# Node stage of a two-layer graph network: a ring of four blocks for the loaded tables, self rows loaded three blocks later, stores eight steps behind

## The chip, the cores and the metric

The kernel runs on one core of one Trainium2 chip. The metric is the device time of one execution in microseconds (us); for the kernel before it is the median of three runs.

## The reference

There are 12,500 nodes with 128 features each and 200,000 edges sorted by destination. Layer 0 adds to x a self branch and a neighbour branch, each relu(row @ W.T + b), normalised over its 128 columns, scaled and shifted; a layer norm follows. Layer 1 gathers projected node rows along the edges, weights them by a small network on the edge attributes, sums them by destination, and mixes them with a projection of the node's own row:

```
def _branch(x, W, b, scale, offset, idx):
    h = relu(x @ W.T + b)
    return (h - mean(h)) * s * rsqrt(var(h) + EPS) + o

# layer 0
feat_neigh = segment_sum(edge_val[:, None] * x[src], dst)
x = layernorm(x + _branch(x, W_self, ..., 0) + _branch(feat_neigh, W_neigh, ..., 1))

# layer 1
sc = x projected by W_sc (own row)       f = x projected by W_l1
g = f[src];  weight = silu-network(edge_scalars)
m = segment_sum(weight * g * edge_attr, dst)
x = layernorm(x + cos(angle(m)) * sc + sin(angle(m)) * (m projected by W_l2))
```

What is changed sits between the two layers: from the summed neighbour rows and the self rows to the new x, sc and f.

## The kernel before, in words

The work is five stages, each a block in which every engine runs its own program; between stages all engines meet at a barrier. (1) Setup and the self stage: 25 blocks of 500 nodes; x plus the self branch goes to `base_scratch` in HBM. (2) The neighbour stage: 196 groups of 1024 edges, summed by scatter-add (indirect DMAs issued by POOL) into four tables in HBM, `sums_scratch0` to `3`. (3) The node stage, lines 718 to 904: the part that the change touches. (4) The edge stage: 196 groups, gathers issued by POOL, sums kept in the SBUF tile `table`. (5) The final stage, 25 blocks.

The node stage treats 25 blocks (NB) of 500 nodes, laid out as 125 partitions by 4 rows (CB) by 128 columns. Every engine runs a software pipeline with `sweep`: eight steps written out, a loop of steps 8 to 23 unrolled by four (UN), the rest written out. In step s an engine works on block s for the first part of the chain and on earlier blocks for the later parts:

- SP, step b: four loads of block b, one from each table, into `t_in` (L761), after a wait on `m_sum` for block b-2; one load of the self rows into `b_in` (L763), after a wait on `m_y` for block b-4; then, for block b-6, a wait on `m_pk` and two stores: x and sc together to `xs_scratch` (L767), f to `f_scratch` (L769).
- PE, step s: adds the four tables of block s by 32 matmul rows against the identity, which also transpose (L799, counts up `m_sum`); the neighbour matmul of block s-1 (L807, L810); the transposes of x of block s-4 (L818, needs `m_x1`); the projection of block s-5 (L825, `m_f`).
- ACT, step s: copies and the relu of those results, and the square roots.
- DVE, step s: statistics of h of block s-2 and of y of block s-3 (after `m_y`), then the two scaled copies of sc and f of block s-5 into `pack` (L894, counts up `m_pk`), then centring of h of block s-2 and of y of block s-3 (L877; the latter writes x into `pack` and counts up `m_x1`).
- POOL, step s: clears `table` once (L776), then for block s-3 scales h (L783) and adds the self rows (L787, `m_y`).

The DMAs of the stage all are issued by SP, in the order of its program; SP stops at each wait. The tile `pack` is a ring of four blocks: before DVE writes x of block m into it in step m+3 (L903), it waits until the stores of block m-4 have landed (L902, semaphores `pk_st`). `done(e, signal, m, n)` makes engine e wait until the signal has been counted up for block m-n; `uses` waits for a ring slot's DMAs. Helpers record some lines: L85, L87 and L89 are the steps of the reciprocal square root.

```
uses(dve, pk_st[i2], r2, 32)
centre(m2, y[:, i2 % 2, :, :], pack[:, i2, :, 0, :], 1).then_inc(m_x1, 1)
```

`dst0` (a copy of the edge destinations, last used in the neighbour stage) and `zeros` (last used in the self stage) are SBUF tiles that stay allocated to the end of the kernel.

Of the kernel before, what the change touches and what calls it, by code (L numbers as in the profile page):

```python
# [13 lines left out]
F32 = mybir.dt.float32  # L14
# [5 lines left out]
P = 128  # L20
N = 12500
E = 200000
D = 128
MUL = 32
EF = 64
TH = 4
# [7 lines left out]
NH = 2 * NSG  # L34
# [3 lines left out]
NP = 125  # L38
CB = 4
NB = N // (NP * CB)  # L40
# [4 lines left out]
NTAB = 4  # L45
NPAD = 99 * P
UN = 4


def sweep(eng, body, first, last, lo, hi):  # L50

    for s in range(first, lo):
        body(s, s // UN, s % UN)
    with eng.Fori(lo // UN, hi // UN) as q:  # L54
        for j in range(UN):
            body(q * UN + j, q, j)
    for s in range(hi, last):
        body(s, s // UN, s % UN)


def at(s, q, j, back):

    return s - back, q + (j - back) // UN, (j - back) % UN
# [7 lines left out]
def done(eng, signal, step, back=0):  # L71

    if not isinstance(step, int) or step >= back:
        eng.wait_ge(signal, step - back + 1)
# [18 lines left out]
def graph_layers(nc, a, out):  # L93
    with ExitStack() as ctx:
        def sb(name, shape, dt=F32):
            return ctx.enter_context(nc.sbuf_tensor(name, shape, dt))

        def sem(name):
            return ctx.enter_context(nc.semaphore(name))

        def bank(name, shape, scope):
            return scope.enter_context(nc.psum_tensor(name, shape, F32))

        base_d = nc.dram_tensor("base_scratch", (N, D), F32, kind="Internal").ap()
# [3 lines left out]
        sums_d = [nc.dram_tensor(f"sums_scratch{i}", (NPAD, D), F32, kind="Internal").ap() for i in range(NTAB)]  # L108
# [2 lines left out]


        dstf = sb("dstf", [P, NH, TH])
        dst0 = sb("dst0", [P, NH, TH])
        base0 = sb("base0", [P, NH])
        base = sb("base", [P, NH])
        base_i = sb("base_i", [1, NH], I32)
# [6 lines left out]
        ident = sb("ident", [P, P])  # L124
# [9 lines left out]
        attr = sb("attr", [NP, NB * CB])  # L134
        attr_s = sb("attr_s", [NP, NB * CB])
        ZPART = NPAD * D // P // (24 // UN)
        zeros = sb("zeros", [P, ZPART])


        with ExitStack() as s0:  # L140
            def tmp(name, shape, dt=F32):
                return s0.enter_context(nc.sbuf_tensor(name, shape, dt))
# [189 lines left out]
        def rows_of(t, b):  # L332
            return t[bass.ds(b * BN, BN), :].rearrange("(c p) d -> p c d", p=NP)

        def live(b):
            return not isinstance(b, int) or 0 <= b < NB
# [161 lines left out]
        with ExitStack() as s2:  # L498
# [24 lines left out]
            ps_n = [bank(f"ps_n{i}", [W, TH, P], s2) for i in range(2)]  # L523
# [191 lines left out]

        table = sb("table", [P, 2, NT])
        with ExitStack() as s3:
            def tmp(name, shape, dt=F32):  # L720
                return s3.enter_context(nc.sbuf_tensor(name, shape, dt))
            b_in = tmp("b_in", [NP, UN, CB, D])
            t_in = tmp("t_in", [NP, 2, NTAB, CB, D])
            nT = tmp("nT", [P, 2, CB, NP])
            h = tmp("h_m", [NP, 2, CB, D])
            y = tmp("y_m", [NP, 2, CB, D])
# [10 lines left out]
            ps_n = bank("ps_mn", [P, CB, P], s3)  # L737
            ps_t = bank("ps_mt", [P, CB, P], s3)
            ps_f = [bank(f"ps_mf{i}", [NP, CB, 2 * D], s3) for i in range(2)]
            b_ld = [sem(f"m_b_ld{i}") for i in range(UN)]  # L740
            pk_st = [sem(f"m_pk_st{i}") for i in range(UN)]
            t_ld = [sem(f"m_t_ld{i}") for i in range(UN)]
            m_sum = sem("m_sum")
# [6 lines left out]
            m_cen, m_hs, m_y, m_x1 = sem("m_cen"), sem("m_hs"), sem("m_y"), sem("m_x1")  # L750
# [3 lines left out]
            with nc.Block() as block:  # L754
                @block.sync
                def _(sp):
                    def body(b, q, j):
                        if live(b):
                            done(sp, m_sum, b, 2)
                            for i in range(NTAB):  # L760
                                sp.dma_start(t_in[:, j % 2, i, :, :], rows_of(sums_d[i], b)).then_inc(t_ld[j], 16)  # L761
                            done(sp, m_y, b, UN)
                            sp.dma_start(b_in[:, j, :, :], rows_of(base_d, b)).then_inc(b_ld[j], 16)  # L763
                        m, r, i = at(b, q, j, 6)
                        if live(m):
                            done(sp, m_pk, m)
                            sp.dma_start(rows_of(xs_d, m),  # L767
                                         pack[:, i, :, 0:2, :].rearrange("p c g d -> p c (g d)")).then_inc(pk_st[i], 16)
                            sp.dma_start(rows_of(f_d, m), pack[:, i, :, 2, :]).then_inc(pk_st[i], 16)  # L769
                    sweep(sp, body, 0, NB + 6, 8, 24)  # L770
                    for i in range(UN):
                        sp.wait_ge(pk_st[i], 32 * len(range(i, NB, UN)))

# [16 lines left out]
                @block.tensor  # L790
                def _(pe):
                    def body(s, q, j):
                        b = s
                        if live(b):
                            uses(pe, t_ld[j], q + 1, 16 * NTAB)
                            done(pe, m_nT, b, 1)
                            for c in range(CB):
                                for i in range(NTAB):
                                    last = pe.matmul(ps_n[:, c, 0:NP], t_in[:, j % 2, i, c, :], ident[0:NP, 0:NP],  # L799
                                                     start=(i == 0), stop=(i == NTAB - 1))  # L800
                            last.then_inc(m_sum, 1)
                        b, r, i = at(s, q, j, 1)
                        if live(b):
                            k = i % 2
                            done(pe, m_nT, b)
                            done(pe, m_relu, b, 2)
                            pe.matmul(ps_m[k][:, :, :], ones[0:1, 0:NP], bias4[:, 1, :, :], start=True, stop=False,  # L807
                                      skip_group_check=True)
                            for c in range(CB):
                                last = pe.matmul(ps_m[k][:, c, :], nT[:, k, c, :], neigh_wT[:, :],  # L810
                                                 start=False, stop=(c == CB - 1), skip_group_check=True)
                            last.then_inc(m_mm, 1)
                        m, r, i = at(s, q, j, 4)
                        if live(m):
                            done(pe, m_x1, m)
                            done(pe, m_x1T, m, 1)
                            for c in range(CB):
                                last = pe.transpose(ps_t[:, c, 0:NP], pack[:, i, c, 0, :], ident[0:NP, 0:NP])  # L818
                            last.then_inc(m_tr, 1)
                        m, r, i = at(s, q, j, 5)  # L820
                        if live(m):
                            done(pe, m_x1T, m)
                            done(pe, m_pk, m, 2)
                            for c in range(CB):
                                last = pe.matmul(ps_f[i % 2][:, c, :], x1T[:, i % 2, c, :], node_w[:, :], start=True, stop=True)  # L825
                            last.then_inc(m_f, 1)
                    sweep(pe, body, 0, NB + 5, 8, 24)
# [434 lines left out]
```

## Time and profile before

| | us |
|---|---|
| median of 3 runs | 6106.29 (6099.2 to 6108.52) |
| the profiled execution's own time | 6105.86 |
| its span | 6104.0 |
| node stage: first load issued, last byte moved | 3300.24, between 3810 and 3812 |
| edge stage: first SP issue | 3814.29 |

| engine | busy us over the span | share |
|---|---|---|
| PE | 3681.6 | 60% |
| DVE | 3027.1 | 50% |
| ACT | 979.0 | 16% |
| POOL | 4237.4 | 69% |

The profile's page has the span in 40 equal slices; the node stage lies in slices 22 to 25. A row of the timeline gives start, duration, engine, line, operation, tiles, and how many like instructions are merged in it (then the duration reaches from the first start to the last end). SPq stands for DMA issues by SP: the duration is what the issue took on SP, not the transfer. The bracket at a row's end is idle time of the engine before it and what ended it.

### The profile page before, as it was taken

Reading aid. Unit: us, or ns where it says so; the run is one execution under the profiler, and the core shown is the slowest. Engines: PE = TensorE matmul, PEld = TensorE weight load, DVE = VectorE, ACT = ScalarE, POOL = GpSimd, SP = SyncE. Lnnn points to the kernel's source line nnn. Section 1 sums busy time; section 2 is a strip of 40 time slices with the busy share of each in tenths; the row PEclk is TensorE's granted clock in tenths of the full one; section 3 lists DMA queues with packets and bytes.
Section 4 is the critical chain, followed back from the end, with each engine's and each line's share of the span. In section 5 each row is a group of like instructions: output and inputs, shape, how many; then the busy total and the mean of one; then the engine's idle time right before and its main releaser. Section 6 shows DMA issues by size and latency. Waiting matters only on the chain. (4 is left out here: it accounts for less than half of the span.)

```text
span 6104.0 us, 77354 instructions
## 1 busy us (share of the span) xinstructions
PE 3681.6 (60%) x19065; PEld 3070.4 (50%) x19065; DVE 3027.1 (50%) x11110; ACT 979.0 (16%) x2389; POOL 4237.4 (69%) x3326
## 2 busy tenths in 40 slices
PE   3455554555445555555453554788888888888841
PEld 2233333333333333333332443788888887887841
DVE  3355555555555555555552544444444444444445
ACT  0122222222222222222220100111111111111100
POOL 1258888888888888888886111777777777777743
PEclk9987666677776676677766777777777777777765
DMA  6356666666666666666664333333333333333322
GB/s 115 139 110 107 107 111 110 107 107 107 109 112 107 107 107 113 109 107 107 107 110 69 103 105 91 80 78 78 76 78 78 76 78 78 76 78 79 76 65 88
DMA packets 841278, 587.30 MB, mean 96 GB/s; under 512 B 333361, under 2 KB 737809, under 8 KB 838161
## 3 DMA queue, kind: packets, MB, share of 16 engines
q0 software_dynamic: 275968, 205.72, 25.4%
q1 hardware_dynamic: 560433, 354.96, 21.1%
q10 hardware_dynamic: 4832, 26.13, 1.1%
q8 instruction: 16, 0.26, 0.0%
q14 instruction: 29, 0.23, 0.0%
HBM read 374.34 MB, written 212.14 MB: 96 GB/s over the span
## 5 line engine op out<-in xcount | busy, mean ns | idle before, releaser
L704 POOL DMA_INDIRECT sums_scratch<-vals,to_i x1568 | 2453.6, 1565 | 513.7 <-issue 358.8
L968 POOL DMA_INDIRECT fg<-f_scratch,src_e x1568 | 1561.7, 996 | 514.5 <-issue 477.5
L650 PE MATMUL ps_n<-same,hot 128*40 128x128 f32 x3136 | 700.2, 417 | 1408.1 <-issue 1406.5
L650 PEld LDWEIGHTS ps_n<-same,hot 128*40 128x40 f32 x3136 | 559.2, 185 | 1512.6 <-issue 1449.2
L997 PE MATMUL ps_eu<-hot,prod 128*128 128x120 f32 x3136 | 906.6, 384 | 0.0
L995 PEld LDWEIGHTS ps_eu<-hot,prod 128*128 128x128 f32 x3136 | 637.2, 249 | 345.6 <-DVE prod L1047 257.2
L995 PE MATMUL ps_eu<-hot,prod 128*128 128x40 f32 x3136 | 629.5, 292 | 290.6 <-DVE prod L1047 290.6
L617 DVE TENSOR_TENSOR to_i<-away,srcf 128x8 int32<-128x8 f32 x196 | 32.9, 168 | 1304.0 <-POOLq L68 1303.8
L1046 DVE TENSOR_TENSOR prod<-ps_ew,fg 128x256 f32<-128x256 f32 x392 | 164.4, 419 | 986.3 <-DMA fg<-f_scratch,src_e 936.2
L997 PEld LDWEIGHTS ps_eu<-hot,prod 128*128 128x128 f32 x3136 | 633.2, 250 | 0.0
L604 DVE SCALAR_TENSOR_TENSOR junk<-srow_s,srcf,lower 128x128 f32<-128x128 int32 x1568 | 581.7, 435 | 0.0
L984 PE MATMUL ps_ew<-fc_w,hid_e 128*128 128x256 f32 x1568 | 498.6, 475 | 22.6 <-DMA hid_e<-hid_scratch 22.6
L663 PEld LDWEIGHTS ps_v<-xw_s,near 40*128 40x128 f32 x3136 | 365.1, 188 | 199.3 <-issue 106.9
L1019 ACT COPY sums_a<-ps_eu 32x80 f32<-32x80 f32 x784 | 170.0, 217 | 1822.3 <-PE ps_eu L997 1815.6
L678 ACT COPY near<-ps_n 40x512 f32<-40x512 f32 x196 | 113.5, 579 | 1910.4 <-PE ps_n L650 1910.4
L984 PEld LDWEIGHTS ps_ew<-fc_w,hid_e 128*128 128x128 f32 x1568 | 368.8, 248 | 81.8 <-DMA hid_e<-hid_scratch 23.0
L663 PE MATMUL ps_v<-xw_s,near 40*128 40x128 f32 x3136 | 402.5, 279 | 1.3 <-ACT vals L689 1.3
L592 DVE TENSOR_SCALAR same<-srow_s,srcf 128x128 f32<-128x128 int32 x1568 | 396.6, 335 | 5.1
L1047 DVE TENSOR_TENSOR prod<-ps_ew,fg 128x768 f32<-128x768 f32 x392 | 371.4, 947 | 0.0
L597 DVE TENSOR_SCALAR hot<-iota_f,rel,ew_s 128x40 f32<-128x40 f32 x1568 | 357.1, 341 | 0.0
L799 PE MATMUL ps_mn<-ident,t_in 125*128 125x125 f32 x800 | 147.0, 366 | 266.1 <-DMA t_in<-sums_scratch 266.1
L783 POOL TENSOR_TENSOR y_m<-h_m,vecs 125x512 f32<-125x512 f32 x25 | 31.5, 1261 | 394.1 <-DVE h_m L877 394.1
(192 smaller groups left out, 4365.6 us busy)
## 6 DMA issues: line engine op xcount, KB each, us to landing
srow_s<-in_src SPq DMA_DIRECT2D x196, 512.0 KB
e_s<-in_edge_attr SPq DMA_DIRECT2D x196, 256.0 KB, 3.8
hid_scratch<-hid SPq DMA_DIRECT2D x196, 256.0 KB, 3.6
hid_e<-hid_scratch SPq DMA_DIRECT2D x196, 256.0 KB
sums_scratch<-zeros ACTq DMA_DIRECT2D x24, 1056.0 KB, 3.9
sums_scratch<-vals,to_i POOLq DMA_INDIRECT x1568, 3.4
fg<-f_scratch,src_e POOLq DMA_INDIRECT x1568
t_in<-sums_scratch SPq DMA_DIRECT2D x100, 250.0 KB
```

The lines of the kernel that those rows point to most:

```text
L592: last = dve.tensor_scalar(same[:, k, t, :], rows[:, t // TH, t % TH, :], srcf[:, t:t + 1], None, ALU.is_equal)
L597: last = dve.tensor_scalar(hot[:, k, t, :], iota_f[:, 0:W], rel[:, t // TH, t % TH:t % TH + 1], ew_s[:, j, t:t + 1], ALU.is_equal, ALU.mult)
L604: last = dve.scalar_tensor_tensor(out=junk[:, t, :], in0=rows[:, t // TH, t % TH, :], scalar=srcf[:, t:t + 1], in1=lower[:, :], op0=ALU.is ...
L650: last = pe.matmul(ps_n[t // TH][:, t % TH, :], hot[:, k, t, :], same[:, k, t, :], start=True, stop=True)
L663: last = pe.matmul(ps_v[t // TH][:, t % TH, :], near[:, k, t, :], xw_s[:, i, t // TH, :], start=True, stop=True)
L704: pool.indirect_dma_start(out=sums_d[i], out_offset=bass.IndirectOffsetOnAxis(ap=to_i[:, j, t:t + 1], axis=0), in_=vals[:, j, t, :], in_of ...
L968: pool.indirect_dma_start(out=fg[:, j, t, :], out_offset=None, in_=f_d, in_offset=bass.IndirectOffsetOnAxis(ap=src_s[:, j, t:t + 1], axis= ...
L984: last = pe.matmul(ps_w[k][:, 2 * t:2 * t + 2, :, :], hid[:, j, t, :], fc2_w[:, :], start=True, stop=True)
L995: pe.matmul(ps_u[k][:, hf, 0, :], prod[:, k, t, 0, :], hot[:, k, t, 0, :], start=(t == 0), stop=False, skip_group_check=True)
L997: last = pe.matmul(ps_u[k][:, hf, 1:4, :], prod[:, k, t, 1, :], hot[:, k, t, 1:4, :], start=False, stop=(t == TS - 1), skip_group_check=True)
L1019: act.copy(sums_a[MUL * c:MUL * (c + 1), i % 2, :, :], ps_u[i % 2][MUL * c:MUL * (c + 1), :, c, :])
L1047: last = dve.tensor_tensor(prod[:, k, :, g, MUL:D].rearrange("p t (d u) -> p t d u", d=3), ps_w[k][:, :, 2 + g, None, :].to_broadcast([P, ...
```

## The change

`t_in` becomes a ring of four blocks instead of two, so the wait in front of the table loads of block b is for the sum of block b-4 instead of b-2. The load of the self rows in step b is now that of block b-3 (its wait: `m_y` of block b-7, four before it). The stores in step b are those of block b-8 instead of b-6, so SP's sweep has two steps more. `pack` and `b_in` keep their four blocks. `dst0` and `zeros` move into a scope that is closed before `table` is allocated, which makes room for the larger `t_in`; this moves SBUF addresses and no instruction. Beside SP's program one index of PE's matmul changes (L799, after: L803).

```diff
-        dst0 = sb("dst0", [P, NH, TH])
...
-        zeros = sb("zeros", [P, ZPART])
+        early = ctx.enter_context(ExitStack())
+        zeros = early.enter_context(nc.sbuf_tensor("zeros", [P, ZPART], F32))
+        dst0 = early.enter_context(nc.sbuf_tensor("dst0", [P, NH, TH], F32))
...
+        early.close()
         table = sb("table", [P, 2, NT])
...
-            t_in = tmp("t_in", [NP, 2, NTAB, CB, D])
+            t_in = tmp("t_in", [NP, UN, NTAB, CB, D])
...
                     def body(b, q, j):
                         if live(b):
-                            done(sp, m_sum, b, 2)
+                            done(sp, m_sum, b, UN)
                             for i in range(NTAB):
-                                sp.dma_start(t_in[:, j % 2, i, :, :], rows_of(sums_d[i], b)).then_inc(t_ld[j], 16)
-                            done(sp, m_y, b, UN)
-                            sp.dma_start(b_in[:, j, :, :], rows_of(base_d, b)).then_inc(b_ld[j], 16)
-                        m, r, i = at(b, q, j, 6)
+                                sp.dma_start(t_in[:, j, i, :, :], rows_of(sums_d[i], b)).then_inc(t_ld[j], 16)
+                        m, r, i = at(b, q, j, 3)
+                        if live(m):
+                            done(sp, m_y, m, UN)
+                            sp.dma_start(b_in[:, i, :, :], rows_of(base_d, m)).then_inc(b_ld[i], 16)
+                        m, r, i = at(b, q, j, 8)
                         if live(m):
                             done(sp, m_pk, m)
                             sp.dma_start(rows_of(xs_d, m),
                                          pack[:, i, :, 0:2, :].rearrange("p c g d -> p c (g d)")).then_inc(pk_st[i], 16)
                             sp.dma_start(rows_of(f_d, m), pack[:, i, :, 2, :]).then_inc(pk_st[i], 16)
-                    sweep(sp, body, 0, NB + 6, 8, 24)
+                    sweep(sp, body, 0, NB + 8, 8, 24)
...
-                                    last = pe.matmul(ps_n[:, c, 0:NP], t_in[:, j % 2, i, c, :], ident[0:NP, 0:NP],
+                                    last = pe.matmul(ps_n[:, c, 0:NP], t_in[:, j, i, c, :], ident[0:NP, 0:NP],
```

Only SP's program is reordered. At the start of the node stage SP's rows read, before (xs_scratch and f_scratch are the stores, t_in the table loads, b_in the self rows):

```order
L761 DMA t_in<-sums_scratch 125x4x128 x4
L763 DMA b_in<-base_scratch 125x4x128
L761 DMA t_in<-sums_scratch 125x4x128 x4
L763 DMA b_in<-base_scratch 125x4x128
L761 DMA t_in<-sums_scratch 125x4x128 [waits m_sum]
L761 DMA t_in<-sums_scratch 125x4x128 x3
L763 DMA b_in<-base_scratch 125x4x128
```

and now:

```order
L763 DMA t_in<-sums_scratch 125x4x128 x16
L767 DMA b_in<-base_scratch 125x4x128
L763 DMA t_in<-sums_scratch 125x4x128 [waits m_sum]
L763 DMA t_in<-sums_scratch 125x4x128 x3
L767 DMA b_in<-base_scratch 125x4x128
```

The table loads of four blocks now go out before the first self row and before the first wait. At the end of the stage, from step 24 (the last table loads) on, SP's rows read before:

```order
L761 DMA t_in<-sums_scratch 125x4x128 [waits m_sum]
L761 DMA t_in<-sums_scratch 125x4x128 x3
L763 DMA b_in<-base_scratch 125x4x128 [waits m_y]
L767 DMA xs_scratch<-pack 125x4x256 [waits m_pk]
L769 DMA f_scratch<-pack 125x4x128
L767 DMA xs_scratch<-pack 125x4x256 [waits m_pk]
L769 DMA f_scratch<-pack 125x4x128
```

with five more such pairs of stores behind them, seven in all; and now:

```order
L763 DMA t_in<-sums_scratch 125x4x128 [waits m_sum]
L763 DMA t_in<-sums_scratch 125x4x128 x3
L767 DMA b_in<-base_scratch 125x4x128 [waits m_y]
L771 DMA xs_scratch<-pack 125x4x256 [waits m_pk]
L773 DMA f_scratch<-pack 125x4x128
L767 DMA b_in<-base_scratch 125x4x128 [waits m_y]
L771 DMA xs_scratch<-pack 125x4x256 [waits m_pk]
L773 DMA f_scratch<-pack 125x4x128
```

with two more groups of three and five pairs of stores behind them: four self rows and nine pairs of stores stand at or behind step 24 where there were one and seven.

## Rows read from the trace of the kernel before

**Rows 1.** The page, part 2: DMA busy tenths and GB/s in 40 slices.

```profile
DMA  6356666666666666666664333333333333333322
GB/s 115 139 110 107 107 111 110 107 107 107 109 112 107 107 107 113 109 107 107 107 110 69 103 105 91 80 78 78 76 78 78 76 78 78 76 78 79 76 65 88
```

**Rows 2.** DMA issues of the node stage: count and KB each.

```profile
t_in<-sums_scratch SPq DMA_DIRECT2D x100, 250.0 KB
xs_scratch<-pack SPq DMA_DIRECT2D x25, 500.0 KB
b_in<-base_scratch SPq DMA_DIRECT2D x25, 250.0 KB
f_scratch<-pack SPq DMA_DIRECT2D x24, 250.0 KB
```

**Rows 3.** Stretches: engines' busy time (instructions), granted PE clock, DMA share, GB/s.

```profile
3302.00:3380.00 78.00, 45.32 (x234) 40.82 (x235) 21.31 (x98) 7.60 (x16) 26.81 (x7) 0.68 0.36 104
3420.00:3740.00 320.00, 162.84 (x864) 139.69 (x864) 153.15 (x591) 29.23 (x80) 42.90 (x34) 0.76 0.35 104
3750.00:3810.00 60.00, 24.41 (x86) 18.13 (x85) 32.23 (x113) 4.84 (x14) 7.58 (x6) 0.68 0.25 76
```

**Rows 4.** Timeline of SP: table loads of steps 1, 2, then of 8 and 24.

```profile
3309.01 9.75 SPq L761 DMA_DIRECT2D t_in<-sums_scratch  x4
3321.34 9.75 SPq L761 DMA_DIRECT2D t_in<-sums_scratch  x4
...
3410.07 11.51 SPq L761 DMA_DIRECT2D t_in<-sums_scratch  x4
...
3725.36 11.55 SPq L761 DMA_DIRECT2D t_in<-sums_scratch  x4
```

**Rows 5.** SP's waits in the node stage: total us, times, longest.

```profile
SPq L767 <- DVE pack L894: 50.1, 7, 10.5
SPq L763 <- POOL y_m L787: 17.4, 9, 2.5
SPq L761 <- PE ps_mn L799: 5.8, 2, 3.6
```

**Rows 6.** Timeline of the end of the stage: SP, PE, DVE.

```profile
3742.84 5.94 PE L799 MATMUL ps_mn<-ident,t_in 125*128 125x125 f32 x32 [9.67 <-DMA t_in<-sums_scratch]
...
3754.40 0.26 SPq L767 DMA_DIRECT2D xs_scratch<-pack  x1
...
3758.94 1.11 DVE L877 TENSOR_SCALAR pack<-y_m,mv_m,rs_m 125x128 f32<-125x128 f32 x4
...
3765.90 0.26 SPq L767 DMA_DIRECT2D xs_scratch<-pack  x1
...
3770.43 1.12 DVE L877 TENSOR_SCALAR pack<-y_m,mv_m,rs_m 125x128 f32<-125x128 f32 x4
...
3776.78 0.26 SPq L767 DMA_DIRECT2D xs_scratch<-pack  x1
...
3788.35 0.27 SPq L767 DMA_DIRECT2D xs_scratch<-pack  x1
...
3789.03 1.12 DVE L877 TENSOR_SCALAR pack<-y_m,mv_m,rs_m 125x128 f32<-125x128 f32 x4
...
3796.06 0.26 SPq L767 DMA_DIRECT2D xs_scratch<-pack  x1
...
3798.03 3.42 SPq L767 DMA_DIRECT2D xs_scratch<-pack  x1
...
3812.26 0.36 DVE L938 COPY base<-base 128x392 f32<-128x392 f32 x1 [14.26 <-PEq L754]
```

**Rows 7.** Stretches of 2 us, same columns as rows 3.

```profile
3750.00:3752.00 2.00, 2.00 (x16) 1.91 (x16) 0.00 (x0) 1.07 (x4) 0.00 (x0) 1.00 0.12 36
...
3754.00:3756.00 2.00, 1.17 (x9) 0.95 (x8) 1.86 (x9) 0.00 (x0) 0.00 (x0) 1.00 0.13 35
3810.00:3812.00 2.00, 0.00 (x0) 0.00 (x0) 0.00 (x0) 0.00 (x0) 0.00 (x0) 0.50 0.23 68
```

## The prediction

> **What bounds the kernel now.** I read the page's slices first, then the node stage by its issues, stretches, SP's waits and its timeline. In the slices the node stage lies where GB/s reads 103, 105 and 91 [rows 1]: about 8% of the span, and the only part whose instructions the change reorders. Its transfers are 25 blocks of four table loads, one self load, one x-and-sc store and one f store, 250 KB each but for the first store's 500 KB [rows 2]. In units of 250 KB (256,000 bytes) that is 8 units a block and 200 in all (the missing 25th f store lies past the stretch that was asked).
>
> The rate is the same whatever the engines do: 104 GB/s while there are only loads, and 104 GB/s over 320 us with stores among them, at a DMA share of 0.36 and 0.35, while PE is busy for half the time [rows 3]. The issues say the same. With loads alone a step of 5 units takes 3321.34 - 3309.01 = 12.33 us, 2.466 us a unit. With stores, 16 steps of 8 units take 3725.36 - 3410.07 = 315.3 us, 19.7 us a step, 2.463 us a unit [rows 4]. So the queue of SP's transfers never runs dry there, and bytes set the pace, not the number of buffers.
>
> A share near 0.36 of 16 engines also says that few engines carry these transfers. The Trainium skill (DMA: Bandwidth & Descriptors, section on why a DMA increments its semaphore by 16 and not by 1) gives a DMA the largest number of engines up to 16 that divides the slowest dimension of both sides, and takes the lowest-numbered ones on the queues of SP and ACT. For 125 partitions that is 5, always the same; 5/16 is 0.31, so the trace nearly agrees, and by that rule too no order of the loads changes the rate.
>
> Only the end of the stage is not full. From 3750 to 3810 the DMAs move 76 GB/s [rows 3]; at 104 those bytes would need 60 × 76/104 = 43.8 us, so they stand still for 16.2 us. The gaps are there to see: 36 GB/s from 3750, 35 from 3754 [rows 7]. The reason is in SP's waits: 50.1 us in 7 waits of the stores for DVE's `pack` [rows 5]. When the last loads are out, six blocks have still to be stored, and `pack` of blocks 19 to 22 comes only every 11 us: 3754.40, 3765.90, 3776.78, 3788.35, then 3796.06 and 3798.03 [rows 6], where a pair of stores takes three units, 7.4 us. So in the tail the chain of the engines is the limit, with holes of 3 to 4 us in the DMA queue, and the last two pairs end the stage: bytes stop near 3811.3 (68 of 104 GB/s in the last 2 us [rows 7]), DVE goes on at 3812.26 [rows 6].
>
> **What the change does, part by part.** Bytes, instructions of PE, ACT, DVE and POOL: unchanged. Cost 0; SP issues the same 175 DMAs, two more empty half-steps. The moved SBUF tiles have no row here; I take 0, and the nearest bound is the spread of the runs, 9 us in all, between 3 us faster and 3 us slower for the median of three.
>
> *Steady steps.* The wait for the sum before the table loads cost 5.8 us in two instances and the wait before the self load 17.4 us in nine [rows 5], all while earlier transfers were still draining at 104 GB/s. Their removal gives 0. That is the point at which deeper buffers usually are expected to pay, and here they can't, below the 2.463 us a unit.
>
> *The end of the stage.* At the end of step 24 SP had issued 182 of the 200 units before (100 table, 25 self, 19 pairs of 3). It now has issued 100 + 22 + 17 × 3 = 173; nine pairs of stores and three self loads follow. I count from one anchor: bytes stop first near 3750.7 [rows 7], with unit 182, and unit n is now done at T(n) = 3750.7 - 2.463 × (182 - n), if the queue doesn't run dry. The last table load is unit 169 instead of 178: T = 3718.7 instead of 3740.8. PE started its sum at 3742.84 [rows 6], 2.0 us behind, so it starts near 3720.7, 22 us earlier. The tail of the engines now runs while the queue still has stores for 31 units, 76 us.
>
> *The wait that takes the place of the old one.* `pack` keeps four slots. DVE may write x of block m only when the stores of block m-4 have landed (L902), and SP now issues those in the step after the one in which DVE wants to write, two steps later than before. Behind that wait in DVE stand the next step's statistics and `pack`; PE's transposes wait for x, and ACT, POOL and PE's next sum stand behind these. In steady steps it costs nothing at the end: DVE waits for the end of SP's step m+4, PE then does the projection and DVE the `pack` of the block before, about 6 us on, while SP wants that `pack` two steps (39 us) later. In the tail I work it out with two lengths of rows 6: from x written (3758.94 + 1.11 = 3760.05) to the next store's issue (3765.90) 5.9 us, and from there to x of the next block (3770.43 + 1.12 = 3771.55) 5.7 us; a load or store lands 2.0 us behind T, and writing x takes 1.1.
> - x of 20: stores of 16 done at T(173) = 3728.5, so x at 3731.6, `pack` of 19 at 3737.5.
> - x of 21: 3743.2 by DVE (3741.5 by the ring, T(177)); `pack` of 20 at 3749.1; x of 22 at 3754.8, `pack` of 21 at 3760.7; x of 23 at 3766.4, `pack` of 22 at 3772.3; x of 24 1.8 us on (3788.35 to 3790.15 before), `pack` of 23 at 3780.0, and of 24 two us on.
> - The queue wants the stores of 20 at T(185) = 3758.1, of 21 at 3765.5, of 22 at 3772.9, of 23 at 3780.3, of 24 at 3787.7. Against 3749.1, 3760.7, 3772.3, 3780.0 and 3782.0, with some 1 us from issue to the first bytes, there is a hole of 0 to 0.7 us at blocks 22 and 23, and none else. Self rows of 22 to 24 now come between the stores, the last at T(182) = 3750.7, before y of 24 is due.
> So the last byte is at T(200) = 3795.0 plus up to 0.7, against 3811.3: 15.6 to 16.3 us earlier. Should the landing be 3 us later than taken, another 3 are lost; should the chain be 0.5 us a step shorter, nothing is gained, because bytes are the floor.
>
> *Start.* `pack` of 0 is wanted in step 8 instead of 6, and t_in of steps 0 to 3 is issued in one go; nothing ran dry there before [rows 3]: 0.
>
> *Sum.* 6105.86 (the profiled execution; 0.43 below the median) - 15.5 = 6090.4; on the median 6106.29 - 15.5 = **6090.8 us**. The edge stage begins 15.5 us earlier and keeps its length.
>
> The Trainium skill (DMA: Bandwidth & Descriptors, the anatomy of one DMA) puts most of a DMA's fixed 2 us into the receipt of the last write, heaviest for HBM. That speaks against this change, since DVE now waits on stores to HBM. The trace has 2.0 us for a load, and under 1 us from the last stored byte to DVE's L938; by the page's 2.0 the steps above stay as they are.
>
> **The rivals.**
> - *The tail stays chain-bound.* If stores land late or the chain is 1 to 2 us longer in each of its five steps, the last `pack` slips by 5 to 10 us beyond the slack and the gain shrinks to 5 to 12 us: 6094 to 6101. For it: the margins at blocks 22 and 23 are under 1 us, and the granted clock of PE is 0.68 over the tail against 0.76 in the loop [rows 3], so a tail that starts elsewhere may meet another clock. Against it: four table loads take SP 9.75 us to issue, as long as their transfers [rows 4], so SP runs ahead of the queue by some transfers, and the steps I took are those of the slower tail.
> - *Nothing gained.* The holes only move: the self rows between the stores, or a ring of `pack` that empties the queue in the loop as much as it fills the tail. 6106. Against it: 39 us of slack.
> - *Slower.* The `pack` ring closes a loop: stores landed, x of the block four on, PE, `pack`, stores. One turn is 1.1 + 5.9 + 7.4 + 2 + 1 = 17.4 us and passes three blocks; it decides only if a turn covers one block, for example because SP, standing in the wait for `pack`, holds back the table loads that PE needs first. Then each of 17 steps would add the issue-to-landing 2 us that no transfer hides: +34 - 15.5 = +18, 6125.
>
> **How the numbers follow.** Forecast 0.78, chain-bound tail 0.12, nothing 0.05, slower 0.05. The bound of 0.2% (12.2 us, what a measurement of this kernel can tell from no change) lies 3.3 us from the forecast, and medians of these runs wander by some 3: of the forecast's 0.78, 0.73 is faster and 0.05 the same; of the chain-bound tail 0.01 is faster and 0.11 the same. Faster 0.74, same 0.21, slower 0.05. The range: 16.3 plus the wander of 6 us below gives 6084; above, it takes in half of the chain-bound tail and reaches 6100.
>
> **What would show it.** Right: 104 GB/s without a gap until about 3795; PE's last sum near 3721; SP's waits for `pack` nearly gone; the first SP issue of the edge stage near 3798 to 3799; steps of 19.7 us in the loop; a new wait of DVE's L877 for stores in steps 7 to 24, without effect. Wrong: any dip of GB/s before 3770 (the ring of `pack` binds), holes of over 1 us after it (the chain still ends last), a step in the loop unlike 19.7 us, or an edge stage that changes its length.

## The result, and the profile after

| | before | after |
|---|---|---|
| median of 18 runs each, us | 6105.99 (6099.2 to 6110.41) | 6114.27 (6112.22 to 6130.2) |
| ratio after / before, 95% interval | | 1.0016 (1.0009 to 1.0023) |
| span of the profiled execution | 6104.0 | 6110.6 |
| up to the first table load of the node stage | 3300.2 | 3300.7 |
| node stage (first issue for `t_in` to first issue for `src_e`) | 514.1 | 512.2 |
| edge stage (to the first issue for `xs_in`) | 2071.5 | 2074.2 |
| last stage (to the end of the span) | 218.2 | 223.5 |

The kernel became 8 us slower, 0.16%, where 15.5 us less were forecast: the wrong sign, and outside the range. Two things happened in one: the node stage gained only 1.9 us, and the last stage, of which no instruction changed, lost 5.3.

The page's slices of after, part 2, beside [rows 1]. The node stage now reads 99, 103, 103 where it read 103, 105, 91: its end is fuller, as forecast, but its middle is emptier. The last two slices fell from 65 and 88 to 63 and 86.

```profile
DMA  6356666666666666666663333333333333333322
GB/s 116 139 109 107 109 111 108 107 107 107 111 110 107 107 110 110 107 107 108 110 111 63 99 103 103 80 76 78 78 77 78 78 77 78 78 78 77 78 63 86
```

SP's timeline of after (start, us, engine, line, operation): the opening table loads, and those of steps 4 and 5, which answer to [rows 4].

```profile
3300.73 39.91 SPq L763 DMA_DIRECT2D t_in<-sums_scratch  x16
...
3343.52 10.88 SPq L763 DMA_DIRECT2D t_in<-sums_scratch  x4
...
3357.03 10.88 SPq L763 DMA_DIRECT2D t_in<-sums_scratch  x4
```

Stretches of after, same columns as [rows 3].

```profile
3302.00:3380.00 78.00, 44.96 (x234) 40.45 (x235) 20.32 (x103) 7.60 (x16) 27.30 (x7) 0.70 0.36 95
3420.00:3720.00 300.00, 178.02 (x803) 146.51 (x802) 111.05 (x540) 31.00 (x75) 36.83 (x30) 0.73 0.36 102
3750.00:3810.00 60.00, 22.63 (x73) 16.44 (x71) 33.14 (x121) 4.26 (x12) 7.58 (x6) 0.67 0.33 106
3780.00:3790.00 10.00, 4.52 (x15) 3.61 (x16) 6.48 (x24) 0.67 (x2) 1.04 (x1) 0.67 0.26 82
5890.00:6090.00 200.00, 27.95 (x92) 21.13 (x92) 108.02 (x429) 4.72 (x23) 65.45 (x69) 0.50 0.29 88
```

The first row is the finding. With loads alone, a step of five units takes 3357.03 - 3343.52 = 13.51 us, 2.70 a unit, where it took 12.33 and 2.466 [rows 4]; the DMAs move 95 GB/s where they moved 104 [rows 3], at the same DMA share of 0.36. The same bytes go by the same queue with the same number of DMAs, and each takes 9.5% longer. In the loop, where five of a block's eight units are loads, 102 GB/s stand for 104. The tail went the way that was forecast, 106 GB/s against 76, with one short dip (82 from 3780). The last stage shows the same as the start: 88 GB/s, against this row of the kernel before:

```profile
5890.00:6090.00 200.00, 29.19 (x96) 22.07 (x96) 112.88 (x440) 4.72 (x23) 68.29 (x72) 0.50 0.29 91
```

SP's and DVE's waits of after (total us, times, longest), beside [rows 5]:

```profile
DVE r_m L877 <- DMA f_scratch<-pack: 184.6, 17, 12.2
...
SPq L771 <- DVE pack L898: 19.2, 5, 7.1
SPq L763 <- PE ps_mn L803: 3.5, 1, 3.5
SPq L767 <- POOL y_m L791: 3.0, 2, 2.2
```

And the timeline of after's tail, beside [rows 6]:

```profile
3737.10 5.72 PE L803 MATMUL ps_mn<-ident,t_in 125*128 125x125 f32 x32 [4.35 <-DMA t_in<-sums_scratch]
...
3796.84 3.01 SPq L771 DMA_DIRECT2D xs_scratch<-pack  x1
...
3810.92 0.36 DVE L942 COPY base<-base 128x392 f32<-128x392 f32 x1 [14.70 <-PEq L756]
```

PE's last sum starts 5.7 us earlier than before, not 22, and the stage ends 1.3 us earlier.

What did change under the loads is their target. In the compiled programs `t_in`, `b_in`, `xs_in` and `o_sb` start in each partition at an address that is 160 over a multiple of 512 bytes before and 288 after (a multiple of 256 plus 160, and plus 32); `pack` went from 64 to 192 and `fg` from 288 to 416, all because `dst0` and `zeros` no longer stand ahead of them.

### The profile page after: what moved, and what is told of

The parts are those of the page before. It is cut to its first block and busy times, and to the rows that moved or that the text cites. A ratio compares the mean times of both kernels' runs of the same rounds, so it can differ in the third digit from the quotient of the medians.

```text
span 6110.6 us, 77374 instructions
## 1 busy us (share of the span) xinstructions
PE 3715.7 (61%) x19065; PEld 3087.4 (51%) x19065; DVE 2989.1 (49%) x11110; ACT 982.9 (16%) x2389; POOL 4242.1 (69%) x3326
## 2 busy tenths in 40 slices
DMA packets 841277, 587.30 MB, mean 96 GB/s; under 512 B 333360, under 2 KB 737808, under 8 KB 838160
## 3 DMA queue, kind: packets, MB, share of 16 engines
q0 software_dynamic: 275968, 205.72, 25.4%
## 5 line engine op out<-in xcount | busy, mean ns | idle before, releaser
L972 POOL DMA_INDIRECT fg<-f_scratch,src_e x1568 | 1563.9, 997 | 513.4 <-issue 477.5
L656 PE MATMUL ps_eh<-eT,fc_w 128*128 128x512 f32 x392 | 307.7, 875 | 0.0
L1044 DVE TENSOR_TENSOR hot<-raw,e_s 128x1280 f32<-128x1280 f32 x196 | 293.3, 1497 | 10.8
```

What stands on the lines that cost most here:

```text
L656: pe.matmul(ps_h[k][:, :, :], fc1_w[:, :], eT[:, k, :, :], start=True, stop=True).then_inc(e_fc1, 1)
L972: pool.indirect_dma_start(out=fg[:, j, t, :], out_offset=None, in_=f_d, in_offset=bass.IndirectOffsetOnAxis(ap=src_s[:, j, t:t + 1], axis= ...
```

## The experiments

All kernels are timed against the kernel before on the same chip. On the chips of the first four sections the edge stage takes 2622 to 2676 us in the kernels profiled there, some 550 to 600 more than in the profile before, and its length follows no edit; so of those runs the stages are compared, and the kernels that matter most are timed once more in the last two sections, where the edge stage takes 2071 to 2074 us. Each row below is read from one profile; "load step" is five loads without stores, "loop step" the mean of the last 15 intervals between table loads, and offsets are the starts of `t_in` and `pack` modulo 512 bytes.

| kernel | t_in, pack | load step | loop step | node stage | last stage | ratio (95%) |
|---|---|---|---|---|---|---|
| before | 160, 64 | 12.33 | 19.74 | 514.1 | 218.2 | 1 |
| after | 288, 192 | 13.50 | 20.12 | 512.2 | 223.5 | 1.0016 (1.0009 to 1.0023) |
| e1_after_160 | 160, 64 | 12.33 | 19.58 | 495.9 | 218.2 | 0.9979 (0.9965 to 0.9993) |
| e4_before_288 | 288, 192 | 13.50 | 20.22 | 530.9 | 223.4 | 1.0042 (1.0026 to 1.0059) |
| e2_after_0 | 0, 416 | 11.77 | 18.81 | 476.5 | 212.7 | 0.9950 (0.9932 to 0.9967) |
| e3_after_0_pack0 | 0, 0 | 11.77 | 18.59 | 473.2 | 212.6 | 0.9944 (0.9926 to 0.9961) |
| e5_order_only | 160, 64 | 12.33 | 19.63 | 495.1 | 218.4 | 0.9969 (0.9955 to 0.9984) |
| e6_ring_only | 160, 64 | 12.33 | 19.60 | 513.5 | 218.4 | 1.0000 (0.9986 to 1.0015) |
| e7_before_0 | 0, 0 | 11.77 | 18.63 | 490.8 | 212.6 | 0.9965 (0.9950 to 0.9981) |
| e9_all_0 | 0, 0 | 11.77 | 18.61 | 474.2 | 212.5 | 0.9919 (0.9897 to 0.9941) |
| e10_order_0 | 0, 0 | 11.77 | 18.49 | 473.8 | 212.6 | 0.9935 (0.9911 to 0.9959) |
| after_again | 288, 192 | 13.50 | 20.13 | 512.5 | 223.5 | 1.0014 (1.0005 to 1.0023) |
| e1_again | 160, 64 | 12.33 | 19.07 | 485.4 | 218.3 | 0.9971 (0.9961 to 0.9981) |
| f1_fg_416 | 160, 64 | 12.33 | 19.74 | 514.1 | 218.1 | 0.9997 (0.9988 to 1.0006) |
| e4_again | 288, 192 | 13.50 | 20.12 | 528.9 | 223.3 | 1.0037 (1.0023 to 1.0051) |
| e9_again | 0, 0 | 11.77 | 18.73 | 476.6 | 212.6 | 0.9926 (0.9912 to 0.9939) |
| e10_again | 0, 0 | 11.77 | 18.70 | 476.5 | 212.5 | 0.9926 (0.9912 to 0.9939) |

### The address alone: e1_after_160, e4_before_288, e2_after_0, e3_after_0_pack0

The first pads the changed kernel so that its tiles lie where they lay before; the second pads the kernel before by 128 bytes, so that they lie where the change puts them. The last two put `t_in` at 0, and then `pack` too.

```diff
+        pad_t = sb("pad_t", [P, 96])      # e1: changed kernel; e2, e3: 56; e4: kernel before, 32
         table = sb("table", [P, 2, NT])
...
+            pad_k = tmp("pad_k", [NP, 24])      # e3 only
             pack = tmp("pack", [NP, UN, CB, 3, D])
```

> The changed kernel with 384 unused bytes per partition ahead of table, so that t_in, b_in, xs_in and pack start at the same offsets within 512 bytes as before the change (160, 160, 160, 64 instead of 288, 288, 288, 192). Theory A (the start address of the SBUF tiles sets the rate of their transfers; the smaller scope for dst0 and zeros moved it): loads at 104 GB/s again, 12.33 us a step of 5 units at the start instead of 13.50, last stage 5 us shorter, in all 6091 us as predicted, 15 to 24 us below the changed kernel. Theory B (the new order or the ring of four itself slows the loads): steps of 13.50 us as in the changed kernel, 6114 us.

> The kernel before with 128 unused bytes ahead of table and nothing else, so that its tiles start where those of the changed kernel start (288, and pack at 192). Theory A: loads alone 13.5 us a step instead of 12.33, loop steps 20.1 instead of 19.7, last stage 5 us longer, in all 6106 + 10 to 25 = 6116 to 6131 us. Theory B: 6106 us, steps of 12.33 and 19.7 us.

> The changed kernel with 224 unused bytes ahead of table: t_in, b_in and xs_in start on a multiple of 512 bytes, pack at 416. If each 512-byte row written costs by the 256-byte pieces that it touches (three at offsets 160 and 288, two at 0), loads get faster than 104 GB/s: with 2 pieces for 3 up to 1.5 times, a step of 5 units 8.2 to 11 us, and the last stage shorter by 10 us or more: 6030 to 6080 us. If only the last 32 bytes at offset 288 were costly, 104 GB/s and 6091 us. Theory B: 6114 us.

> As the run with t_in on a multiple of 512 bytes, and 96 more unused bytes ahead of pack, which then starts on a multiple of 512 too. If the source address counts for stores as the target address for loads, the three units of stores in a loop step get cheaper as well: another 1 to 2 us on each of 17 steps, 17 to 34 us. If it does not count, the same time as that run. Theory B: 6114 us.

The load step follows the offset and nothing else: 12.33 at 160 and 13.50 at 288 with either program. With the old addresses the new order takes 495.9 us for the stage, 18.2 less than before. The kernel before at the new ones takes 530.9, 16.8 more, and is 0.42% slower with no instruction changed. At 0 the step is shorter than either, 11.77 us (2.354 a unit), so 160 had never been good. The last stage goes by it as well: 218.2, 223.4 and 212.7. Moving `pack` from 416 to 0 gave 3.3 us in the stage, and 0.9944 against 0.9950, which the intervals do not tell apart; two profiles of one program differ as much (e10: 473.8 and 476.5). Both sizes expected of the last two were missed: the load step was to be 8.2 to 11 us, and `pack` at 0 was to give 17 to 34 us.

### The two halves of the change: e5_order_only, e6_ring_only, e7_before_0, e9_all_0

The first keeps the kernel before, every address included, and writes SP's body in the new order; the second keeps the ring of four at the old addresses and writes SP's body in the old order. The third is the kernel before with `t_in` and `pack` at 0. The fourth is the changed kernel with every tile that is loaded or stored in bulk at a multiple of 512 bytes.

```diff
 # e5, in the kernel before
-                            done(sp, m_y, b, UN)
-                            sp.dma_start(b_in[:, j, :, :], rows_of(base_d, b)).then_inc(b_ld[j], 16)
-                        m, r, i = at(b, q, j, 6)
+                        m, r, i = at(b, q, j, 3)
+                        if live(m):
+                            done(sp, m_y, m, UN)
+                            sp.dma_start(b_in[:, i, :, :], rows_of(base_d, m)).then_inc(b_ld[i], 16)
+                        m, r, i = at(b, q, j, 8)
...
-                    sweep(sp, body, 0, NB + 6, 8, 24)
+                    sweep(sp, body, 0, NB + 8, 8, 24)
 # e6: the reverse of these lines in the changed kernel, with pad_t of 96
 # e7, in the kernel before: pad_t of 88, pad_k of 24
 # e9, in the changed kernel: pad_t of 56, pad_k of 24, and pads of 88 words behind dst0,
 #     24 ahead of res, 120 ahead of vals, 96 ahead of fg
```

> The kernel before with only the new order of SP: self rows of block b-3 and stores of block b-8 in step b, t_in still a ring of two, no address moved. Theory A1 (the order fills the end of the stage, the ring is idle): node stage (first table load to first issue of the edge stage) 496 us as in the changed kernel at the old offsets, against 514 before; time 18 us below the kernel before. Theory A2 (the ring of four is needed to bring the last loads forward): 510 to 514 us, no gain.

> The changed kernel at the old offsets, but with SP's old order: t_in a ring of four, self rows of block b and stores of block b-6 in step b. Theory A1: node stage 514 us as before, no gain. Theory A2: 496 us.

> The kernel before (order and ring of two) with t_in, b_in, xs_in and pack on multiples of 512 bytes. Theory A (offset sets the rate, order sets the holes, independently): loads alone 11.77 us a step of 5 units, last stage 212.6 us; node stage 473 us plus the 18 us of holes that the new order fills = 489 to 493 us, since the tail of the engines does not get shorter with faster transfers; time 27 to 31 us below the kernel before. If faster transfers take the holes with them: 473 us.

> The changed kernel with every tile that SP or POOL moves in rows of 512 bytes on a multiple of 512: x_in and res of the self stage, vals of the neighbour stage, t_in, b_in and pack, fg of the edge stage, xs_in and o_sb of the last. Theory A: node stage 473 us, last 212.6 us as with t_in and pack there already; self stage shorter by up to 25 x 2 x 0.11 = 5 us if its transfers are a limit; the two stages that POOL's indirect DMAs pace unchanged (POOL's issues are back to back), so 40 to 46 us below the kernel before. If the offset also sets the pace of the indirect DMAs, which carry most of the bytes: over 60 us below.

The order alone gives it all: 495.1 us, 19.0 less than before, and 0.9969. The ring of four alone gives nothing: 513.5 and 1.0000, and SP's waits for `pack` are as they were, as e6's row shows beside [rows 5]:

```profile
SPq L770 <- DVE pack L897: 50.7, 7, 10.5
```

The address alone takes 23.3 us off the stage (e7, 490.8), and order and address add up: 514.1 - 19.0 - 23.3 = 471.8, against 474.2 measured for e9. At offset 0 the order gives 490.8 - 474.2 = 16.6. On e9 its expectation has a slip: the indirect DMAs do not carry most of the bytes (205.72 of 587.30 MB in the kernel before).

### How the rate goes by the offset: s0_64, s32_64, s256_32

At this point two accounts of the offset stood against each other, called P and Q in the expectations. Each of these three kernels was profiled once and is not timed against the kernel before; each gives the four slots of `t_in` four different starts, by padding a slot; the opening 16 loads then show four offsets in one profile.

```diff
-            t_in = tmp("t_in", [NP, UN, NTAB, CB, D])
+            t_raw = tmp("t_in", [NP, UN, NTAB * CB * D + 16])   # s256_32: 8
+            t_in = t_raw[:, :, 0:NTAB * CB * D].rearrange("p j (i c d) -> p j i c d", i=NTAB, c=CB)
 # pad_t: 56 (s0_64: 0, 64, 128, 192), 64 (s32_64: 32, 96, 160, 224), 120 (s256_32: 256, 288, 320, 352)
```

> The changed kernel with 64 unused bytes behind each of the four slots of t_in: the slots start at 0, 64, 128 and 192 within 256 bytes. The first 16 transfers of the node stage fill slots 0 to 3, four each, and the issues of SP show their pace. Known: 2.354 us a transfer at 0, 2.466 at 160, 2.70 at 288 (32 within 256). Theory P (256-byte pieces touched): 2.354 at 0, and a slower, common pace at 64, 128 and 192. Theory Q (multiples of 64 are whole): 2.354 at all four.

> As the run with slots at 0, 64, 128 and 192, moved by 32 bytes: 32, 96, 160, 224. If the pace depends on the offset within 256 bytes, 2.70 us at 32 as at 288; 2.466 at 160. Theory P: 96 and 224 as 64 to 192. Theory Q: all slower than 2.354.

> Slots at 256, 288, 320 and 352 within 512 bytes. If only the offset within 256 counts: 2.354 us at 256, 2.70 at 288, and 320 and 352 as 64 and 96 in the other two runs. If 512 counts, 256 is slower than 0.

Stretches in which the loads of one slot were on their way; the last column is GB/s. First s0_64, offsets 0, 64, 128, 192:

```profile
3301.00:3309.00 8.00, 0.00 (x0) 0.00 (x0) 0.00 (x0) 0.00 (x0) 8.00 (x1) 0.50 0.36 108
3311.00:3319.00 8.00, 5.41 (x32) 5.22 (x31) 0.00 (x0) 0.57 (x1) 8.00 (x1) 0.76 0.36 101
3321.00:3328.00 7.00, 7.00 (x40) 6.12 (x41) 0.00 (x0) 0.57 (x1) 0.00 (x0) 0.76 0.36 108
3331.00:3338.00 7.00, 5.24 (x38) 4.17 (x37) 0.00 (x0) 2.28 (x3) 0.00 (x0) 1.00 0.38 100
```

s32_64, offsets 32, 96, 160, 224:

```profile
3300.00:3308.00 8.00, 0.00 (x0) 0.00 (x0) 0.00 (x0) 0.00 (x0) 8.00 (x1) 0.50 0.36 97
3311.00:3318.00 7.00, 5.31 (x30) 5.12 (x29) 0.00 (x0) 0.57 (x1) 7.00 (x1) 0.71 0.36 104
3321.00:3328.00 7.00, 7.00 (x38) 6.12 (x37) 0.00 (x0) 0.58 (x1) 0.00 (x0) 0.69 0.36 104
3331.00:3339.00 8.00, 4.89 (x35) 3.82 (x34) 0.79 (x5) 2.66 (x4) 0.00 (x0) 1.00 0.38 95
```

s256_32, offsets 256, 288, 320, 352:

```profile
3304.00:3312.00 8.00, 0.00 (x0) 0.00 (x0) 0.00 (x0) 0.00 (x0) 8.00 (x1) 0.50 0.35 107
3315.00:3322.00 7.00, 5.43 (x28) 5.24 (x26) 0.00 (x0) 0.57 (x1) 7.00 (x1) 0.65 0.36 95
3325.00:3332.00 7.00, 7.00 (x35) 6.12 (x33) 0.00 (x0) 0.58 (x1) 0.00 (x0) 0.63 0.36 99
3335.00:3342.00 7.00, 5.75 (x42) 4.68 (x41) 0.33 (x4) 1.77 (x3) 0.00 (x0) 1.00 0.37 104
```

Both accounts fell, for 128 is as good as 0, and 64 is not. The rates repeat after 256 bytes (0 and 256, 32 and 288) and are the same on either side of a multiple of 256 (96 and 160: 104; 64 and 192: 101 and 100; 32 and 224: 97 and 95). A row of 512 bytes that starts off a multiple of 256 is cut by two such boundaries into a short piece, 256 bytes, and the rest; the rate goes by the shortest piece: 107 to 108 GB/s where it has 128 bytes or none is short, 104 with 96, 99 to 101 with 64, 95 to 97 with 32. In time for a load of 250 KB that is 2.354, 2.466 and 2.700 us at none, 96 and 32: some 0.115 us more for every 32 bytes that are missing to 128. It looks as if a piece of under 128 bytes cost about as much as one of 128, which by bytes would be 6% more for 96 and 19% more for 32, where 4.8% and 14.7% are measured. So the rule by the offset is measured for loads of such rows, and its reason is only argued.

The Trainium skill (DMA: Bandwidth & Descriptors, section on how a descriptor splits into AXI transactions) has transactions cut at multiples of 256 bytes, with the bytes from the boundary below the start up to the start fetched for nothing and counted in beats of 32 bytes. The cut and the period of 256 agree with the runs. The price doesn't: by its beats a start at 160 wastes five and one at 32 only one, while the runs have 2.466 us a unit at 160 and 2.700 at 32. The page tells of a descriptor's read, and here the odd start is on the side that is written.

### Order without the ring, at good addresses: e10_order_0

e5 with `pad_t` of 88 and `pad_k` of 24 words.

> The kernel before with SP's new order alone (t_in a ring of two, dst0 and zeros where they were) and t_in, b_in, xs_in and pack on multiples of 512 bytes. By theory A the two effects add: node stage 473 us, last stage 212.6 us, 40 us below the kernel before, as with the ring of four. If the faster loads need the ring: node stage 480 us or more.

473.8 us for the stage: as good as with the ring of four (e3 473.2, e9 474.2).

### The sum again, and the edge stage: after_again, e1_again, f1_fg_416

The changed kernel and e1_after_160 again, and the kernel before with `fg` alone moved to where the change puts it (`pad_f` of 32 words ahead of it).

> The changed kernel itself, once more, beside the kernel before and its version at the old offsets on one chip. By theory A (order and offsets add): node stage 512 us, last stage 223.5 us, 2 to 8 us above the kernel before in the time (node -2, last stage +5, edge stage unclear).

> The changed kernel at the old offsets, once more: node stage 496 us, last stage 218.2 us, 18 us below the kernel before and 21 to 26 us below the changed kernel on the same chip. If the edge stage too pays for the moved tiles, the difference of the two edge stages shows 3 us or more, where that stage is steady enough to see it.

> The kernel before with 128 unused bytes ahead of fg, which then starts at 416 within 512 bytes, as in the changed kernel, instead of 288; node and last stage untouched. If the 2.7 us that the edge stage grew come from the place of fg, the edge stage is 3 us longer than in the kernel before. By the law of the slots (288 costs more than 416) it should get shorter, not longer, if that law holds for the gathers; if the gathers do not care, no difference.

The address costs the changed kernel 6113.05 - 6085.32 = 27.7 us, and without it the change is what the forecast said in sign, 0.9971. The edge stage's 2.7 us is no effect: with `fg` at 416 it takes 2072.4 us and the ratio is 0.9997, and the six profiles of this section and the next have 2070.5 to 2074.3, whatever the kernel. In e1_again the node stage takes 485.4 us, 10.6 less than expected, because its loop steps take 19.07 us. Its timeline:

```profile
3341.62 9.93 SPq L764 DMA_DIRECT2D t_in<-sums_scratch  x4
3353.95 9.93 SPq L764 DMA_DIRECT2D t_in<-sums_scratch  x4
...
3712.19 5.47 PE L804 MATMUL ps_mn<-ident,t_in 125*128 125x125 f32 x32 [4.49 <-DMA t_in<-sums_scratch]
...
3785.53 0.36 DVE L943 COPY base<-base 128x392 f32<-128x392 f32 x1 [14.71 <-PEq L757]
```

12.33 us for a load step again; and DVE goes on 26.7 us earlier than in [rows 6]. In the loop it moves 108 GB/s, where the kernel before moves 104 [rows 3] at the same offsets. The tail still has one hole, 76 GB/s over 10 us:

```profile
3420.00:3690.00 270.00, 166.66 (x766) 136.57 (x764) 106.08 (x520) 29.80 (x73) 35.41 (x28) 0.73 0.35 108
...
3760.00:3770.00 10.00, 6.29 (x24) 4.78 (x22) 4.73 (x13) 0.57 (x1) 0.00 (x0) 0.83 0.25 76
```

### The versions that beat both: e4_again, e9_again, e10_again

e4, e9 and e10 once more.

> The kernel before with 128 unused bytes ahead of table (t_in, b_in, xs_in at 288, pack at 192), once more, on a chip whose edge stage is not held by its gathers. Theory A: node stage 531 us (+17), last stage 223.4 us (+5), and what the changed kernel's edge stage adds: 22 to 25 us above the kernel before, the mirror image of the 21 to 28 us that the changed kernel loses to its own version at the old offsets.

> The changed kernel with all tiles that move in rows of 512 bytes on multiples of 512, once more: node stage 473 us (-41), last 212.6 us (-5.6), self stage -5: 50 us below the kernel before, 6056 us. If only these three stages count and the edge stage is as before.

> The kernel before with SP's new order alone and t_in, b_in, xs_in and pack on multiples of 512 bytes, once more: node stage 474 us (-40), last 212.6 us (-5.6), self stage as before: 46 us below the kernel before, 6060 us.

e4 again loses 0.37% by an address alone. e9 and e10 take 6059.91 and 6060.21 us against 6106.45: 46 us less than before, 0.74%, some 53 less than the changed kernel. The first stretch of e9_again has 109 GB/s, and its last stage 94:

```profile
3297.00:3330.00 33.00, 18.42 (x112) 16.29 (x113) 1.42 (x9) 2.33 (x4) 17.97 (x1) 0.76 0.36 109
5890.00:6040.00 150.00, 23.11 (x76) 17.48 (x76) 90.16 (x349) 3.69 (x18) 51.67 (x55) 0.50 0.29 94
```

e10 is the simpler of the two: the old ring of two, SP's new order, and two pads. The other pads of e9 show no gain in the time over it, and its edge stage, where `fg` now starts at 0, takes 2071.7 us as elsewhere.

## Why the prediction was wrong, step by step

- *The step that failed* is the sentence "The moved SBUF tiles have no row here; I take 0", with 3 us either way as its bound. The runs show 27.7 us in its place (after_again against e1_again), the largest term of all. In the profiles of these two it is 27.1 us in the node stage and 5.2 in the last. By the price of a load, 125 loads of a unit × (2.700 - 2.466) would be 29.3 us. After against e1_after_160 it is 512.2 - 495.9 = 16.3 and 5.3: there the loop steps of e1_after_160 take 7.25 us beyond the load step and those of after 6.62, which takes 19 × 0.6 = 12 off the 29.3 (below). The bound failed with the value: 3 us was taken from how the medians wander, which says nothing of what a different address does.
- *"The rate is the same whatever the engines do", so bytes set the pace.* Right that the queue never runs dry in the loop, and the reason why the miss was dear: a stage bound by its transfers pays for each one that gets longer. But the rate of 104 GB/s was taken as the queue's own; it was that of loads at offset 160. Stores alone move at 117 to 118 (below), so the 104 with stores among the loads was a coincidence, and e1_again has 108 there.
- *Steady steps: removal of the waits gives 0.* Right: e6 has the deeper ring and 1.0000.
- *The end of the stage, -15.5.* Right in mechanism at the old addresses, and near in size: -18.2 (e1_after_160) and -19.0 (e5). PE's last sum, forecast near 3720.7, starts at 3719.48 in e1_after_160 and 3722.57 in e5. E1_again gained 28.7 in the stage, of which 16 × (19.74 - 19.07) = 10.7 are loop steps, which no term of the forecast had. Two terms of the sum in the tail were off and partly cancel: with the queue full, stores and self rows move faster there than 2.463 us a unit (117 GB/s over 3740 to 3750 in e1_again), which fits a queue that empties sooner and a hole that is longer than worked out; and DVE goes on 0.7 to 1.8 us after the last packet of the stores that it waits for (after and e1_again), where 2.0 was taken. The count "nine pairs of stores" behind step 24 is a slip for eight; the units, 173 and 27 more, are right.
- *SP's waits for `pack` nearly gone.* Half: 19.2 us in 5 waits, where there were 50.1 in 7 [rows 5]; 19.6 in 5 in e1_again. The holes are there (82 and 76 GB/s over 10 us), longer than the 0.7 us worked out: in e1_again no packet starts for 1.6 us, from 3761.3 to 3763.0. That is a part of the first rival, the chain-bound tail. It did not shrink the gain below the forecast.
- *The new wait of DVE is harmless.* Right: 17 times, 184.6 us in all; e1_after_160 has 175.7 us of it and e1_again 168.0, and both are faster than before.
- *The rivals.* "Slower", by a ring of `pack` that adds 2 us to each step, did not happen; the loop step of after did get 0.4 longer, but it is 19.6 or less with the same order and ring at the old addresses, and 20.2 with the old order at the new ones (e4). "Nothing gained" named a time, 6106, that is closer than the forecast's, for a cause that isn't there: that is luck.
- *The edge stage keeps its length*: yes, within its spread. That the last stage would keep it as well, taken without a word, was wrong.

The sum of what the profiles show for the change, -1.9 in the node stage and +5.3 in the last, is +3.4; the median moved by 8.3 (6.6 when timed again). The remaining 3 to 5 us are not placed: they are within what the stages before and the edge stage differ by from profile to profile (3297.0 to 3304.6, without e9, and 2070.5 to 2074.3 us).

What a loop step takes beyond its load step, 6.6 to 7.4 us, goes with no simple rule of the offset of `pack`: 7.25 to 7.41 at 64, but 6.74 in e1_again; 6.62 to 6.72 at 192; 6.72 to 6.96 at 0. Loads and stores are mixed there. But the tails have stretches of 10 us in which the queue is full and holds stores alone. In the order e1_again (`pack` at 64), after_again (192), e2 (416) and e10_again (0):

```profile
3741.00:3751.00 10.00, 4.51 (x12) 3.22 (x12) 7.91 (x30) 0.87 (x3) 2.52 (x2) 0.56 0.34 118
...
3768.00:3778.00 10.00, 3.74 (x12) 2.89 (x12) 8.54 (x34) 0.87 (x3) 2.53 (x2) 0.66 0.35 117
...
3729.00:3739.00 10.00, 4.51 (x12) 3.21 (x12) 7.91 (x32) 0.87 (x3) 2.52 (x2) 0.54 0.34 118
...
3733.00:3743.00 10.00, 4.51 (x12) 3.21 (x12) 7.92 (x32) 0.87 (x3) 2.53 (x2) 0.54 0.34 118
```

So stores go at one rate at these four starts, and `pack` needs no pad for their sake. The packets of the traces show one thing more: the first table load behind a store pays little for its offset. In the loop of after_again it takes 2.5 us, where the other four loads of a step take 2.7. So an offset costs less in the loop than in a step of loads alone.

It stays open why loop steps at 160 and 64 take up to 0.7 us more in some profiles than in e1_again. The same program has 19.58 us in e1_after_160 and 19.07 in e1_again, on two chips; but f1_fg_416, with the old order on the chip of e1_again, has 19.74, so the chip alone doesn't explain it. By the packets most of the difference lies in the f store and the first load behind it (2.57 and 2.60 us against 2.44 and 2.41), while the queue has work throughout.

## What to carry to other kernels

Where a profile says that transfers set the pace, the time of one transfer is a number to be explained, not a constant: write down where its SBUF tile starts, before and after, and treat an allocation that moves as a change of every DMA into the tiles behind it. Start tiles that are loaded in rows of 512 bytes at multiples of 128 bytes, by a pad if need be; here the pads of e7 gave as much as the reordering (e5), and both together twice that. And when an edit that moves instructions also moves addresses, the first experiment is the one with a pad that holds the addresses still.

## What the runs showed of the hardware that was not expected

- Loads of 512-byte rows from HBM to 125 partitions run at 107 to 108 GB/s with an SBUF start of 0 or 128 modulo 256, 104 at 96 or 160, 99 to 101 at 64 or 192, 95 to 97 at 32 or 224. The DMA share reads 0.35 to 0.38 for all of them: the share doesn't show that a transfer is slow.
- Stores from `pack` move at 117 to 118 GB/s with a start of 0, 64, 192 or 416 modulo 512.
- Unused bytes in front of the tiles, with no instruction changed, make this kernel 0.4% slower (128 bytes, e4) or 0.35% faster (352 bytes, and 96 ahead of `pack`, e7).
- The edge stage takes 2071 to 2074 us on some chips and 2622 to 2676 on others, with one program, and the reason stays open. In the kernel before POOL issues the gathers of `fg` almost back to back (idle for 514.5 us in front of them, 477.5 of it "issue"); in e1_after_160 it is idle for 1028.4, 531.7 of it in waits for DVE's `prod`, so it is on the chips of this second kind that the gathers do not set the pace, and not, as the expectation of e4_again has it, on those of the first. The last stage of one program is alike on both to 0.1 us, the node stage to 2 or 3 us, but for e1_after_160 (495.9) and e1_again (485.4).
